# An attention pipeline: projections cut in halves, and q and k transfers moved ahead in the SP queue

## The reference

```python
def _L0_attn_ref(x, ...):                    # 8 x 512 x 256, 16 heads of 16
    q, k, v = x @ Wq.T + bq, x @ Wk.T + bk, x @ Wv.T + bv
    attn = softmax(q @ k / sqrt(16)) * head_mask
    return (attn @ v) @ Wo.T + bo

def _L0_ffn_ref(x, ...):
    h = x + _attention(_rmsnorm(x, g1), wq, wk, wv, wo)   # causal, rotary
    return h + _moe(_rmsnorm(h, g2), w_router, wg, wu, wd)

x = _layernorm(x + _L0_attn_ref(x, ...))
x = _layernorm(x + _L0_ffn_ref(x, ...))
```

## Time and profile before

| what | value |
|---|---|
| time, median of 3 runs | 1469.72 us (1464.93 to 1469.98) |
| the profiled execution | 1469.85 us, its span 1468.1 |
| PE, DVE, ACT, POOL busy | 87%, 65%, 57%, 54% of the span |
| first exponential of step 0, of step 63 | 91.4 us, 871.5 us |
| a plain unit, steps 16 to 19 | 50.6 us |
| a causal unit, mean of steps 36 to 55 | 49.8 us |

### The profile page before, as it was taken

One profiled execution on the slowest core, in us unless ns is written; L12 is line 12 of the kernel. 1 busy time (PEld: TensorE's weight loads), 2 busy tenths in 40 slices (PEclk: granted clock), 3 DMA queues, 4 the chain that ended last, 5 costly groups with the idle time before them and its releaser, 6 DMA issues. The chain is left out here.

```text
span 1468.1 us, 33103 instructions
## 1 busy us (share of the span) xinstructions
PE 1280.0 (87%) x11455; PEld 707.7 (48%) x11456; DVE 950.6 (65%) x1764; ACT 830.1 (57%) x1672; POOL 796.7 (54%) x835
## 2 busy tenths in 40 slices
PE   1799999999989998998999993369999999999990
PEld 0222223232323444444444432358888888888880
DVE  6478888888998787778888721834444444444443
ACT  3148787888888776666676671124444433344334
POOL 2322565475547657566645234146666666666654
PEclk9769999999999999899999895579999999999995
DMA  4416667676767878687867433855232222223326
GB/s 127 87 36 173 178 174 208 187 195 189 186 189 222 218 208 224 201 214 202 209 161 176 115 98 109 255 182 133 45 47 43 43 43 50 43 43 47 45 31 236
DMA packets 159005, 204.45 MB, mean 139 GB/s; under 512 B 31217, under 2 KB 121329, under 8 KB 158897
## 3 DMA queue, kind: packets, MB, share of 16 engines
q1 hardware_dynamic: 141424, 182.55, 45.1%
q0 software_dynamic: 17472, 20.50, 8.8%
HBM read 111.46 MB, written 82.87 MB: 132 GB/s over the span
## 5 line engine op out<-in xcount | busy, mean ns | idle before, releaser
L1006 ACT ACTIVATE a_probs<-a_ps_s 128x512 f32<-128x512 f32 (+2 forms) x896 | 460.4, 569 | 167.1 <-PE a_ps_s L801 161.9
L1075 DVE TENSOR_REDUCE a_shift_max<-a_ps_m 128x1 f16<-128x512 f32 x512 | 320.4, 682 | 70.4 <-PE a_ps_m L806 69.0
L806 PE MATMUL a_ps_m<-a_qkx 48*128 48x128 f16 (+3 forms) x1408 | 286.4, 303 | 18.7 <-DVE a_shift_max L1075 8.9
L1632 PE MATMUL e_ps_gu<-e_xT,w_up 128*128 128x256 f16 x2574 | 298.2, 274 | 1.7 <-ACT e_xT L1686 1.4
L801 PE MATMUL a_ps_s<-a_qkx 49*128 49x128 f16 (+3 forms) x1408 | 277.7, 298 | 14.9 <-ACT a_probs L1006 14.8
L1632 PEld LDWEIGHTS e_ps_gu<-e_xT,w_up 128*128 x2574 | 250.0, 98 | 34.9 <-issue 5.4
L902 PE MATMUL a_ps_o<-a_probs,a_v_one 128*32 128x512 f32 (+3 forms) x2048 | 235.5, 533 | 2.8 <-ACT a_o L1013 2.7
L801 PEld LDWEIGHTS a_ps_s<-a_qkx 49*128 49x128 f16 x1408 | 90.7, 95 | 268.7 <-ACT a_probs L1006 155.8
L1568 POOL DMA_INDIRECT h<-e_y,e_put x78 | 125.5, 1609 | 87.9 <-DVE e_y L1728 67.9
L553 POOL TENSOR_TENSOR a_o_half<-a_o_half,a_inv_half 128x512 f32<-128x512 f32 x32 | 41.1, 1286 | 229.5 <-DMA a_inv_half<-a_inv_dram 229.5
L1740 DVE TENSOR_TENSOR e_h<-e_gate,e_ps_gu 128x512 f32<-128x512 f32 (+2 forms) x156 | 82.6, 550 | 126.0 <-ACT e_gate L1694 107.2
(11 more groups left out here) (194 smaller groups left out, 1662.9 us busy)
## 6 DMA issues: line engine op xcount, KB each, us to landing
a_qkx<-a_qk_dram SPq DMA_DIRECT2D x192, 128.0 KB, 4.3
a_qk_dram<-a_qk SPq DMA_DIRECT2D x32, 512.0 KB, 5.2
a_o_dram<-a_o SPq DMA_DIRECT2D x64, 256.0 KB, 2.9
a_o_half<-a_o_dram SPq DMA_DIRECT2D x32, 256.0 KB
a_inv_half<-a_inv_dram SPq DMA_DIRECT2D x32, 256.0 KB
part<-a_part SPq DMA_DIRECT2D x16, 512.0 KB, 5.7
a_q_swap<-a_q SPq DMA_DIRECT2D x64, 128.0 KB
a_w_in<-in_wg SPq DMA_DIRECT2D x16, 352.0 KB, 5.0
```

The lines of the kernel that those rows point to most:

```text
L806: return pe.matmul(out, qx[first:first + 48, r, pair, q * P:(q + 1) * P], kx[first:first + 48, r, pair, k0:k1], start=start, stop=stop)
L1006: act.activation(dst, src, ACT.Exp).then_inc(exp_out, 1)
L1075: vector.tensor_reduce(out, src, AX.X, ALU.max, negate=True).then_inc(max_out, 1)
L1632: mm = pe.matmul(ps_gu[:, bank, kind, f % 2], w[:, ds(e, 1)].rearrange("p o f -> p (o f)"), xT[:, s, xh, k, :], start=n == 0, stop=n == 5)
```

## The change

Each heavy piece is cut into two halves, one in the middle of each of two successive quarters: `piece_at(n, 2)` now runs over quarters 0 and 1, `piece_at(n, 3)` over quarters 2 and 3. Light pieces go to the end of quarters 1 and 3, and are emptied at the start of the quarter behind. In SP's queue the plain layer's `store_qk` moves from the end of the odd step to the even step ahead of it, `load_qk` from the even step to the start of the odd step ahead of it; in the causal layer `load_qk` moves ahead of `swap`, and `store_qk` ahead of the weights. POOL does `factors` and `split_x` ahead of the split of q and k.

```diff
@@ piece_at
-            (1, 0): ("parts", u - 3, 1), (1, 1): ("rows", u, 1), (1, 2): ("qk", u + 2, 0), (1, 3): ("qk", u + 2, 1),
+            (1, 0): ("rows", u, 1), (1, 1): ("parts", u - 3, 1), (1, 2): ("qk", u + 2, 0), (1, 3): ("qk", u + 2, 1),
...
-        for i in range(4):
+        for i in (2, 0, 3, 1):
@@ sync
                 if n % 2 == 0:
-                    swap((n + 6) // 2)
-                    load_qk((n + 4) // 2)
+                    if causal((n + 4) // 4):
+                        load_qk((n + 4) // 2)
...
                     store_o(n - 1)
+                    swap((n + 6) // 2)
                     for m in weights_at(n - 1):
                         store_weights(m)
                         load_weights(m + 2)
+                    if plain((n + 6) // 4):
+                        store_qk((n + 6) // 2)
                     load_o(n // 2 - 1)
                 else:
+                    if plain((n + 5) // 4):
+                        load_qk((n + 5) // 2)
                     load_rows((n + 1) // 2)
                     store_inv((n - 3) // 2)
...
                     load_inv((n - 3) // 2)
+                    if causal((n + 5) // 4):
+                        store_qk((n + 5) // 2)
                     for m in weights_at(n - 1):
                         store_weights(m)
                         load_weights(m + 2)
-                    store_qk((n + 5) // 2)
@@ tensor: project (project_v and project_out in the same way)
+                products = [(wh, xh, k) for wh, xh in ((0, 0), (0, 1), (1, 0)) for k in range(KD)]
+                for n in range(3 * j, 3 * j + 3):
+                    wh, xh, k = products[n]
...
+            def half_piece(n, quarter):
+
+                j = quarter % 2
+                piece = piece_at(n, 2 + quarter // 2)
...
+            def light_piece(n, quarter):
+
+                piece = piece_at(n, quarter // 2) if quarter % 2 else None
...
-                    a_piece(n, quarter)
+                    half_piece(n, quarter)
...
                         weigh(n, quarter - 2)
+                    light_piece(n, quarter)
@@ scalar
+            def empty_light(n, quarter):
+                piece = piece_at(n, 0) if quarter == 2 else piece_at(n - 1, 1) if quarter == 0 else None
...
-                    early = (1 if quarter < 2 else 0) if causal(u) else 3
+                    early = 0 if causal(u) and quarter >= 2 else 1
+                    empty_light(n, quarter)
```

More of the change, by code:

```diff
@@ L634, in _ @@
                         part_low(u - 2)
+                    if plain(h // 2):
+                        split_high(h)
+                        split_low(h)
                     turn_half(h)
@@ L675, in piece_done, with project @@
                 mm.then_inc(piece_mm, 1)
-            def project(u, c):
+            def project(u, c, j):
                 layer = u // B
-                if plain(u):
-                    pe.wait_ge(xT_hi, u + 1)
-                    pe.wait_ge(xT_lo, u + 1)
-                else:
-                    emptied_piece(pe, "turn", u, 1)
-                w, m = c % 2, c // 2
-                n = 0
-                for wh, xh in ((0, 0), (0, 1), (1, 0)):
+                if j == 0:
+                    if plain(u):
+                        pe.wait_ge(xT_hi, u + 1)
+                        pe.wait_ge(xT_lo, u + 1)
+                    else:
+                        emptied_piece(pe, "turn", u, 1)
+                w, m = c % 2, c // 2
+                products = [(wh, xh, k) for wh, xh in ((0, 0), (0, 1), (1, 0)) for k in range(KD)]
+                for n in range(3 * j, 3 * j + 3):
+                    wh, xh, k = products[n]
+                    mm = pe.matmul(ps_x[:], t.w_proj[:, 4 * layer + w, wh, k, m * P:(m + 1) * P],
+                                   xT[:, u % 2, xh, k, :], start=n == 0, stop=n == 5)
+                if j == 1:
+                    piece_done(mm, "qk", u, c)
@@ L688, in project, with project_v @@
+            def project_v(u, i, j):
+                layer = u // B
+                n, q = 0, 2 * i + j
+                for wh, xh in ((0, 0), (1, 0), (0, 1)):
                     for k in range(KD):
-                        mm = pe.matmul(ps_x[:], t.w_proj[:, 4 * layer + w, wh, k, m * P:(m + 1) * P],
-                                       xT[:, u % 2, xh, k, :], start=n == 0, stop=n == 5)
+                        mm = pe.matmul(ps_x[:, j * D:(j + 1) * D], xT[:, u % 2, xh, k, q * P:(q + 1) * P],
+                                       t.w_proj[:, 4 * layer + 2, wh, k, :], start=n == 0, stop=n == 5)
@@ L691, in project @@
                         n += 1
-                piece_done(mm, "qk", u, c)
-            def project_v(u, i):
-                layer = u // B
-                for j in range(2):
-                    n, q = 0, 2 * i + j
-                    for wh, xh in ((0, 0), (1, 0), (0, 1)):
-                        for k in range(KD):
-                            mm = pe.matmul(ps_x[:, j * D:(j + 1) * D], xT[:, u % 2, xh, k, q * P:(q + 1) * P],
-                                           t.w_proj[:, 4 * layer + 2, wh, k, :], start=n == 0, stop=n == 5)
-                            n += 1
-                piece_done(mm, "v", u, i)
+                if j == 1:
+                    piece_done(mm, "v", u, i)
@@ L761, in a_piece @@
                 kind, u, k = piece
-                if numbers[piece] > 0:
-                    pe.wait_ge(piece_out, numbers[piece])
+                if j == 0:
+                    free_piece(piece)
                 if kind == "qk":
-                    project(u, k)
+                    project(u, k, j)
                 elif kind == "v":
-                    project_v(u, k)
-                elif kind == "turn":
+                    project_v(u, k, j)
+                else:
+                    project_out(u, k, j)
+            def light_piece(n, quarter):
+                piece = piece_at(n, quarter // 2) if quarter % 2 else None
+                if piece is None:
+                    return
+                kind, u, k = piece
+                free_piece(piece)
+                if kind == "turn":
                     turn_x(u, k)
@@ L963, in move_parts, with empty_piece @@
                 act.activation(nT[:, 0].rearrange("p k s -> p (k s)"), ps_x16[:], ACT.Copy).then_inc(piece_out, 1)
-            def empty_piece(n, i):
-                piece = piece_at(n, i)
+            def empty_piece(n, quarter):
+                piece = piece_at(n, 2 + quarter // 2) if quarter % 2 else None
                 if piece is None:
@@ L973, in empty_piece @@
                     move_v(u, k)
-                elif kind == "rows":
+            def empty_light(n, quarter):
+                piece = piece_at(n, 0) if quarter == 2 else piece_at(n - 1, 1) if quarter == 0 else None
+                if piece is None:
+                    return
+                kind, u, k = piece
+                if kind == "rows":
                     move_rows(u, k)
@@ L1214, in _ @@
                 for quarter in range(4):
-                    early = causal((n + 3) // G)
+                    empty_light(n, quarter)
                     for i in range(4):
```

50 lines of the change are left out of this document (24 added, 26 removed).

## The result

The changed kernel takes **1634.56 us**, the median of 4 runs (1632.23 to 1635.05), against 1469.85 us for the kernel before beside it (4 runs, 1464.93 to 1474.81): ratio 1.1117, 95% interval 1.1079 to 1.1156. The direction was forecast; 164.7 us slower instead of 62 was not, and the time lies outside the range.

What follows compares the result with a forecast made beforehand. No engine alone was taken as the bound: uneven quarters run engines dry in turn, beside the chain from rows to aT. 1469.85 + 40 (plain) + 17 (causal) + 5 (clock) = 1532 us, range 1466 to 1576.

Steps and rivals of the forecast that it cites:

- What bounds the kernel: Attention stage: no engine idle for long, uneven quarters run engines dry in turn; rows to aT take 11.0 us.
- Halves: Both layers: plain quarter needs 2.78 us of PE, plain unit gains 3.6 to 47.0; causal unit stays 46.5 at best.
- "About nothing is lost" for xT: Query and key projections need xT two quarters sooner; POOL's new order gives it 3.2 us sooner.
- The loop: Plain layer: q/k transfers ahead of rows and reciprocals close a loop through SP and POOL; unit 58.4 us, layer +40.
- The out wait, plain: Out projection moved forward in group 2: PE waits 4.6 us for aT, plain unit 51.6 instead of 50.6.
- The out wait, causal: Causal out projection: wait of 5.7 us on 46.5 gives 52.2 a unit against 49.8, seven units, +17.
- Queue, causal: SP, causal layer: earlier q/k store and load, later swaps, counted at nothing; swaps bounded by some 3 us per step.
- The clock: PE's granted clock: one more slow step from longer waits, +5; bounds none and +51.
- rival 3: PE's clock falls at every wait: 1578 us, chance 0.12.
- Rivals 1, 2 and 4: Whole kernel: 1 out wait without loop, 1493, chance 0.22; 2 faster, 1440, 0.12; 4 nothing measurable, 1470, 0.09.

Runs made afterwards that it cites:

- e4: Changed kernel with SP's queue order of before and out projections whole in their old quarters; 1494.57 us, ratio 1.0212 to the kernel before.
- e1: Changed kernel with SP's queue order of before, halves and POOL's new order kept; 1593.42 us.
- e9: Kernel before with halves only in plain steps of groups 0 and 3, units 0 to 5; 1467.84 us, ratio 1.0017.
- e2: Kernel before with SP's and POOL's new orders alone, all pieces whole and in their old quarters; 1553.60 us.
- e6: Kernel before with SP's new order alone, POOL's order as before; 1516.96 us.
- e7: Kernel before with both new orders in the plain layer only, but the q/k load behind rows and reciprocals; 1481.66 us.
- e11: Kernel before with the out projection alone cut in halves and moved forward two quarters, in both layers; 1545.89 us.
- e8: Kernel before with only the four swaps of an even causal step moved behind the output store; 1515.72 us.
- e10: Changed kernel with 20 needless matmuls ahead of the wait for aT, before the first out piece only; 1627.91 us.

## Why the prediction was wrong in size

The forecast was 62 us, the result 164.7. In the plain layer 83.5 came where 40 stood, in the causal one 80.6 where 17 stood; the 5 for the clock belong to both. The wait for `aT` and the loop were there as forecast. What failed are terms of the sum: in the loop the link from the rows to the reciprocals' load, the gain of the halves, the causal unit without its wait, the causal queue put at nothing, and the clock.

- **What bounds the kernel.** Right. PE has little idle time, quarters differ, and the chain from rows to `aT` decides.
- **Halves.** Right for a quarter of plain groups 0 and 3: an even one takes 2.84 us, forecast 2.78. Wrong for their worth: step 16 takes 12.00 us where 11.1 stood, and with the two other edits undone (e4) the plain layer takes 5.7 more than before, where 3.6 less in each unit was forecast. In the causal layer "PE has no hole to fill", costed at nothing, was wrong by 19.3 (e4): the light pieces' bank is emptied later there, and PE waits 15.9 us for it.
- **"About nothing is lost" for xT.** Right where nothing else delays POOL (2.4 us in e1's plain layer). In the change the loop holds POOL up, and PE waits 3.38 us in step 17; that lies beside the loop, since SP sends the rows at 351.97 because of its queue, which the q/k load fills until 351.92, and not of PE. What I left out is the neighbour of this operand: shorter steps make the q/k load late (e1, e9).
- **The loop.** Right in kind: e2, e6 and e7 show it, and each of the two links that close it. Its size was too small, 65.1 us a unit instead of 58.4; over steps 8 to 23, its four full turns, the change takes 58.0 more than before (260.1 for 202.1) where 31 stood. Of the links, with their forecasts: PE from the out projection to the rows 18.67 (302.45 to 321.12) for 17.05, as the clock is low behind the wait; rows to the reciprocals' load 5.12 in one half and 8.01 in the other (351.97 to 359.98) for 2.85; the q/k store's landing 2.95 for 5.22; POOL from `aT` to the end of the split 12.1 for 12.0. These sum to +6.9 of the 7.1 by which 302.45 to 367.94 exceeds the forecast's 58.4. The step that failed: I bounded the landings of the large transfers from above by their rows, and gave the 16 KB store none of its own, since before it landed in 1.5 us with only an output store beside it. Behind 768 KB of loads it took up to 6.7, and e7, with the loads behind it, gives at most 2.7. The Trainium skill (DMA: Bandwidth & Descriptors, Queues, rings and completion order) says that each DMA engine takes a ring's descriptors in order and lets a semaphore's increment land only after its earlier writes. The 6.7 agrees with that. The Trainium skill's fit that the prediction names (same page, Anatomy of one DMA — SWDGE (gpsimd) path) is for that path, while the profile lists SP's transfers under a hardware queue. Its estimate of 3.2 us for the q/k store lies near the 2.95 measured after SP had stood still, that of 2.6 for the reciprocals' load far below the 4.64 of the row.
- **The out wait, plain: 4.6, so 51.6 a unit, +1.0.** The wait itself was nearly right: in e1, which has no loop, PE waits 34.8 us in seven units, 5.0 each. The sum around it failed. The 3.6 that the halves were to give back did not come, and of the 42.3 by which e1 exceeds e4 15.7 are longer PE busy time, the clock behind the wait, which I had priced apart as one step's 5. Alone on the kernel before the move costs 25.0 (e11).
- **The out wait, causal: +17.** Right place, wrong size: 47.3 alone (e11). The wait was forecast as 5.7 and is shorter, 4.70 in step 50 and 27.4 over eight steps of the layer (35.0 in e11). But I added it to an undisturbed 46.5, as if it took the place of what already made a unit 49.8; in the kernel before PE waits only 6.0 us in all for `aT`, so the wait is not the whole of that; what else it is was not looked for. The clock behind the wait adds 2.5 a unit in e11 (20.1 over eight).
- **Queue, causal: "at nothing".** The largest term without a price. The swaps alone cost 37.4 (e8), the whole new queue 29.5 alone (e2) and 22.5 within the change. I named the cover ("the rest of the step") and bounded its loss at 3 us a step, which the 37.4, over 13 even steps, just keeps, but left the bound out of the range. The true cover was the landing of the q/k store.
- **The clock: +5, at most +51.** It rose to 48.4 us of PE busy time, about what rival 3 had priced. Its mechanism happened: the granted clock falls behind 14 of the 15 waits. The Trainium skill (TensorE: Matmul & The Clock Gate, What's actually happening) has the clock throttled by default and released by activity, and the trace agrees in step 50 in so far as the 0.50 follows a wait and ends while PE works. Rival 3 is not the reason for the size by itself: with all 48.4 taken off, the change would still stand at 1586, and 115.7 are idle time. What the clock is worth in time stays open, as e10 gave 36.1 of it back for a gain of 6.7 with a filler that was 11.1 too long.
- **Rivals 1, 2 and 4.** The loop is there, so not 1, although the landing of the q/k store did shrink as 1 asked; the link from rows to the reciprocals' load grew by more. The chain grew rather than shrank, so neither 2 nor 4.

## What to carry to other kernels

A queue that issues in order is a set of covers: before a transfer is moved, write down which landing it now fills, and price that landing bare. A wait put ahead of a second wait can close a loop through another engine, and then the period of the loop, not any engine's busy time, is the time of a stage. Cut a heavy piece in halves only where its operand is early, then look which transfer has become late: the halves paid here, by 0.5%, only once the store of q and k moved too.

## What was not expected of the hardware

- The 16 KB store landed after 1.9 to 6.7 us, median 4.3, behind six loads of 128 KB on the same queue; after 1.4 to 1.5 us in the kernel before and 1.4 to 2.7 in e7, where the loads stand behind it.
- One wait of 4.70 us was followed by 14.7 us at 1.2 GHz although PE was full in them (4.37 of 4.40, 5.09 of 5.50, 4.77 of 4.80 us); waits of 6.66 to 8.04 us in the plain layer were followed by 3 to 6 us.
- Returning most of the clock returned little time: 36.1 us less of PE busy, 6.7 us less in all, with a filler that made the waits 11.1 us longer.
